# Attention softmax: the scaling of P by the inverse row sums, on ScalarE in place of VectorE

## The chip, the cores and the metric

One core of a Trainium2 chip. The metric is the device time of one execution in microseconds. All times below are of this kernel on this chip.

## The reference

The model is a "macaron" layer on 4 sequences of 256 tokens with hidden size 512: half a feed-forward step, attention, half a feed-forward step, each on a layer-normed input and added to x.

```python
x = x + 0.5 * ffn(layernorm(x))      # dense 512x512 + bias, LoRA with 8 experts of rank 16, top 2
x = x + attn(layernorm(x))           # 32 query heads, 8 key/value heads of 128, window of 128, rope
x = x + 0.5 * ffn(layernorm(x))
...
scores = einsum('bqhgd,bshd->bhgqs', qg, k) * sm_scale
allowed = (j <= i) & (j > i - 128)
attn = softmax(where(allowed, scores, neg), axis=-1)
out = einsum('bhgqs,bshd->bqhgd', attn, v).reshape(B, S, N_Q_HEADS * HEAD_DIM) @ wo
```

The part that the change touches is the division inside `softmax`: each row of exponentials is scaled by the inverse of its sum.

## The kernel before

Everything is fp32. To keep precision on a matrix engine that rounds its operands, each operand is split in a "hi" part (a rounded copy, made by ScalarE) and a "lo" part (the difference, made by VectorE or GpSimd), and each product is made of three passes.

**Loops.** The attention runs over 8 groups g (one key/value head with its 4 query heads). Each group has two halves (two sequences each), and each half 8 slots s: sequence b and query head h. That makes 128 units u. In a slot one head of one sequence goes through the softmax. Since the window is 128 and a sequence has two tiles of 128 queries, P of a unit is two tiles of 128x128: for the first query tile the causal block, for the second the causal block and the previous block folded in one by taking the element-wise minimum, because their allowed places don't overlap.

**Order of the work.** Nothing is scheduled by a tool: each engine has its own instruction list, written out slot by slot in a function `group(g, first, last)` of that engine, and runs it strictly in order. Semaphores tie the engines. The lists are skewed by a unit. In slot s, with u its unit:

- TensorE: nine matmuls of the next half's projections (`project`), `scores(u + 1)`, `p_transpose(u - 1)`; in slots 1 and 5 also `values`, in slots 2, 3, 6 and 7 `out_project`.
- VectorE: in slot 0 `v_lo`; in slots 0, 3, 4 and 7 `x_add`; then `softmax_norm(u)`; `rope_sum` and `rope_cos` in the slots in which a projection ends; `p_lo(u - 1)` (L827); `softmax_min(u + 1)` (L805 to L813); in slots 1 and 5 `o_lo`.
- ScalarE: `softmax_exp(u)` (L549, two exponentials of 128x128 with their row sums); in slot 0 `v_hi`; weight copies (`split_hi`, L495), before the rest in slots 4 and 7 of the first half, and some at the end of slots; `rope_swap` (L523, two copies of 64x512) in slots 1, 2, 3, 5 and 6, `v_copy` in slot 7; `p_hi(u - 1)` (L557); in slots 1 and 5 `o_hi`; then `rope_hi`.
- GpSimd: `rope_sin` (L365), `p_part(u - 1)` (L372, released by `p_lo`), `rope_lo` (L382), and weight differences (`split_lo`, L357), four of them for wo after slot 4 of the first half.
- SP issues the weight loads, each released by the differences that free its buffer.

The projections of a half end in slots 1, 2, 3, 5, 6 and 7, and that is where rope work of the list above stands.

**Around the change.** `exp_done`, `rinv_done` and `norm_done` count units. `p_transpose` waits for `norm_done`, `softmax_min(u + 1)` reads scores and writes `sm`, and the next `softmax_exp` waits for `min_done`. `prob`, `sm`, `rsum`, `rinv` and `nmax` have two buffers, taken by s % 2.

Of the kernel before, what the change touches and what calls it, by code (L numbers as in the profile page):

```python
# [22 lines left out]
ACT = mybir.ActivationFunctionType  # L23

P = 128
# [50 lines left out]
def macaron(nc, x_in, wq, wk, wv, wo, w_base, b_base, w_router, lora_a, lora_b, ident_in, mask_in, side_in, rope_in, out):  # L76
    ctx = ExitStack()
    with ctx:
# [29 lines left out]
        prob = sb("prob", [P, 2, 3 * P])  # L108
# [8 lines left out]
        rinv = sb("rinv", [P, 2, 2])  # L117
# [75 lines left out]
        rinv_done, norm_done = sem("rinv_done"), sem("norm_done")  # L193
# [242 lines left out]
        def _(act):  # L436
# [108 lines left out]
            def softmax_exp(u, s):  # L545
# [5 lines left out]
                                                accum_out=rsum[:, s % 2, i:i + 1])  # L551
                last.then_inc(exp_done, 1)

            def p_hi(u, s, beta):
                act.wait_ge(t_done, u + 1)
                wait(act, pv_done, 2 * beta)
                nc.scalar.activation(pT[0][:, 0:2, s % G, :], T[:, 0:2 * P].rearrange("p (c n) -> p c n", c=2),  # L557
                                     ACT.Copy).then_inc(pthi_done, 1)
# [8 lines left out]
            def group(g, first, last):  # L567
                for hf in range(2):
                    for s in range(SLOTS):
                        u, beta, b = 16 * g + 8 * hf + s, 4 * g + 2 * hf + s // G, s // G  # L570
                        start = first and hf == 0
                        softmax_exp(u, s)
                        if s == 0:
                            v_hi(2 * g + hf, hf)
                        weights(g, hf, s, last, (0, 1))
                        split, m = (ENDS.get(c) if not (last and hf == 1) else None for c in (s - 1, s))
                        if m == 5:
                            v_copy(2 * g + hf + 1)
                        elif m is not None:
                            rope_swap(2 * g + hf + 1, m)  # L580
                        if not (start and s == 0):
                            p_hi(u - 1, s - 1, beta - (s % G == 0))
                        if last and hf == 1 and s == 3:
                            x_hi(2, 0)
                            x_hi(2, 1)
                        if s % G == 1 and not (start and b == 0):
                            o_hi(beta - 1, (b + 1) % 2)
                        if split is not None and split < 5:
                            rope_hi(2 * g + hf + 1, split, 1 - hf)
                        weights(g, hf, s, last, (2, 3))  # L590
# [66 lines left out]
        def _(dve):  # L657
# [155 lines left out]
                nc.vector.tensor_tensor(sm[:, s % 2, P:2 * P], sm[:, s % 2, P:2 * P], sm[:, s % 2, 2 * P:3 * P],  # L813
                                        ALU.min).then_inc(min_done, 1)

            def softmax_norm(u, s):
                dve.wait_ge(exp_done, u + 1)
                nc.vector.reciprocal(rinv[:, s % 2, :], rsum[:, s % 2, :]).then_inc(rinv_done, 1)  # L818
                dve.wait_ge(rinv_done, u + 1)
                for i, (lo, hi) in enumerate(((0, P), (P, 2 * P))):  # L820
                    last = nc.vector.tensor_scalar(prob[:, s % 2, lo:hi], prob[:, s % 2, lo:hi],  # L821
                                                   rinv[:, s % 2, i:i + 1], None, ALU.mult)
                last.then_inc(norm_done, 1)

            def p_lo(u, s):
                dve.wait_ge(pthi_done, u + 1)
# [31 lines left out]
            def group(g, first, last):  # L858
                for hf in range(2):
                    for s in range(SLOTS):  # L860
                        u, beta, b = 16 * g + 8 * hf + s, 4 * g + 2 * hf + s // G, 2 * hf + s // G
                        start = first and b == 0
                        split, m = (ENDS.get(c) if not (last and hf == 1) else None for c in (s - 1, s))
                        if s == 0 and not (last and hf == 1):
                            v_lo(2 * g + hf, hf)
                        if s % G == 3 and not start:
                            x_add(beta - 1, (b - 1) % BATCH, 0)
                        if s % G == 0 and not (first and b < 2):
                            x_add(beta - 2, (b - 2) % BATCH, 1)
                        softmax_norm(u, s)  # L870
                        if split is not None and split < 5:
                            rope_sum(2 * g + hf + 1, split)
                        if m is not None and m < 5:
                            rope_cos(2 * g + hf + 1, m)
                        if not (start and s == 0):
                            p_lo(u - 1, s - 1)
                        if m == 5:
                            v_diff(2 * g + hf + 1)
                        if s == 0 and last and hf == 1:
                            v_lo(2 * g + hf, hf)  # L880
                        if not (last and hf == 1 and s == SLOTS - 1):
                            softmax_min(u + 1, (s + 1) % SLOTS)
                        if s % G == 1 and not start:
                            o_lo(beta - 1, (b + 1) % 2)
                        if last and hf == 1:
                            ffn_start(s)
# [415 lines left out]
```

## Time and profile before

| | us |
|---|---|
| median of 3 runs | 777.33 (776.9 to 781.51) |
| the profiled execution | 778.18 |
| its span, first to last instruction | 776.5 |
| TensorE, VectorE, ScalarE, GpSimd busy | 731.0, 643.7, 411.2, 392.9 |
| clock granted to TensorE, mean | 0.987 of full speed |

The profile is of one execution. Its time is 1.7 us longer than the span, for what lies before the first and behind the last instruction. A busy share is time with an instruction on the engine; matmuls overlap in the record, so a busy TensorE is not one at its peak. The attention stage runs from the first exponential at 96.31 us to the last at 725.94.

### The profile page before, as it was taken

The numbers are of one execution on the slowest core, as the hardware profiler recorded it, in microseconds if no ns is written. First come the engines' busy times: TensorE is split into PE (matmuls) and PEld (weight loads), VectorE is DVE, ScalarE is ACT, GpSimd is POOL, SyncE is SP. The second block draws the span as 40 slices with busy tenths as digits, with TensorE's granted clock in tenths as the row PEclk, the third lists the DMA queues.
The fourth block names the chain that finished last, engine by engine and source line by source line (L and its number), as shares of the span: only waits on it lengthen the run. The fifth ranks groups of instructions, "written<-read, shape, count | busy, mean of one in ns | idle before, by whom it ended". The sixth has DMA issues, their size and how long they took to land.

```text
span 776.5 us, 13949 instructions
## 1 busy us (share of the span) xinstructions
PE 731.0 (94%) x3692; PEld 606.8 (78%) x3692; DVE 643.7 (83%) x2060; ACT 411.2 (53%) x1122; POOL 392.9 (51%) x466
## 2 busy tenths in 40 slices
PE   5989878999899999999999999998999899988998
PEld 3878667888788877887788788887888788876876
DVE  3888879888888898878888888888878888898795
ACT  1333456655665566556565656565656655554311
POOL 0384537643764375537653665357634764462420
PEclk8899998999999999999999999999999999999999
DMA  9040002200210022001200120002100210020002
GB/s 298 1 177 14 1 0 69 69 1 1 68 56 14 0 68 54 14 0 54 68 14 0 30 80 24 0 5 90 41 0 0 73 49 0 2 109 0 1 29 82
DMA packets 25843, 32.13 MB, mean 41 GB/s; under 512 B 5833, under 2 KB 14281, under 8 KB 25298
## 3 DMA queue, kind: packets, MB, share of 16 engines
q1 hardware_dynamic: 21072, 30.43, 12.3%
q10 hardware_dynamic: 4738, 1.31, 0.8%
q8 instruction: 14, 0.23, 0.1%
q14 instruction: 19, 0.16, 0.1%
HBM read 27.54 MB, written 4.19 MB: 41 GB/s over the span
## 4 chain that ended last, share of the span: by engine, by line
PE 47%; DVE 31%; issue 10%; ACT 9%; ACTq 2%; DVEq 1%; POOL 0%
PE bank L1101 16%; PE bank L1159 12%; DVE sm L813 7%; PE bank L1144 5%; PE bank L1067 4%; ACT prob L549 4%; PE bank L1123 3%; DVE sm L806 3%; DVE rot L777 3%; DVE oT_lo L833 2%; DVE rot L786 2%; DVE pT_hi_lo L827 2%; DVE sm L805 2%; PE bank L1131 2%; ACTq L442 2%
## 5 line engine op out<-in xcount | busy, mean ns | idle before, releaser
L549 ACT ACTIVATE prob<-sm,nmax 128x128 f32<-128x128 f32 x256 | 101.1, 396 | 220.2 <-DVE sm L813 217.7
L365 POOL TENSOR_TENSOR swap<-swap,rope 128x512 f32<-128x512 f32 x80 | 104.9, 1311 | 151.2 <-ACT swap L523 151.2
L372 POOL TENSOR_SCALAR_AFFINE_SELECT pT_hi_lo<-pT_hi_lo 128x256 fp32r<-128x256 f32 x128 | 52.8, 413 | 145.8 <-DVE pT_hi_lo L827 145.0
L813 DVE TENSOR_TENSOR sm<-sm 128x128 f32<-128x128 f32 x128 | 112.1, 876 | 0.0
L523 ACT ACTIVATE swap<-bank 64x512 f32<-64x512 f32 x160 | 95.1, 594 | 9.5 <-PE bank L1101 6.7
L382 POOL TENSOR_TENSOR q_lo<-rot,q_hi 128x512 fp32r<-128x512 f32 x64 | 82.6, 1291 | 7.6 <-ACT q_hi L531 7.6
L821 DVE TENSOR_SCALAR prob<-prob,rinv 128x128 f32<-128x128 f32 x256 | 78.9, 350 | 4.5
L1159 PE MATMUL bank<-wo_hi,oT_hi 128*128 128x512 f32 x256 | 75.1, 415 | 5.0 <-DVE x L840 4.6
L1101 PE MATMUL bank<-xnT_hi,wq_hi 128*128 128x512 f32 x256 | 73.0, 398 | 2.9 <-DVE v_lo L797 1.3
L1101 PE MATMUL bank<-xnT_lo,wq_hi 128*128 128x512 f32 x256 | 73.9, 391 | 0.0
L1101 PE MATMUL bank<-xnT_hi,wq_lo 128*128 128x512 f32 x256 | 72.3, 395 | 0.0
L1159 PE MATMUL bank<-wo_lo,oT_hi 128*128 128x512 f32 x256 | 68.8, 390 | 0.0
L1159 PE MATMUL bank<-wo_hi,oT_lo 128*128 128x512 f32 x256 | 68.6, 390 | 0.0
L777 DVE TENSOR_TENSOR rot<-bank,rope 128x512 f32<-128x512 f32 x80 | 54.9, 687 | 12.9 <-ACT swap L523 12.9
L557 ACT ACTIVATE pT_hi_lo<-bank 128x256 fp32r<-128x256 f32 x128 | 48.9, 382 | 29.6 <-PE bank L1131 22.7
L1144 PE MATMUL bank<-pT_hi_lo,v_hi 128*128 128x512 f32 x192 | 62.1, 404 | 0.0
L1101 PEld LDWEIGHTS bank<-xnT_hi,wq_hi 128*128 128x128 f32 x256 | 47.8, 189 | 16.0 <-DVE rot L777 4.5
L818 DVE RECIPROCAL rinv<-rsum 128x2 f32<-128x2 f32 x128 | 20.6, 161 | 47.0 <-ACT prob L549 47.0
L827 DVE TENSOR_TENSOR pT_hi_lo<-bank,pT_hi_lo 128x256 fp32r<-128x256 f32 x128 | 53.4, 417 | 6.2 <-ACT pT_hi_lo L557 5.9
L1123 PE MATMUL bank<-k_hi_lo,q_hi 128*128 128x256 f32 x256 | 58.3, 310 | 0.0
L786 DVE TENSOR_TENSOR rot<-rot,swap 128x512 f32<-128x512 f32 x80 | 57.2, 716 | 0.0
L1159 PEld LDWEIGHTS bank<-wo_lo,oT_hi 128*128 128x128 f32 x256 | 48.1, 188 | 10.8
(148 smaller groups left out, 1724.1 us busy)
## 6 DMA issues: line engine op xcount, KB each, us to landing
raw<-in_L_attn_wq SPq DMA_DIRECT2D x32, 256.0 KB, 3.0
raw<-in_L_attn_wo SPq DMA_DIRECT2D x32, 256.0 KB, 2.7
x<-in_L_attn_x SPq DMA_DIRECT2D x4, 512.0 KB, 7.8
raw<-in_L_attn_wk SPq DMA_DIRECT2D x8, 256.0 KB, 2.6
raw<-in_L_attn_wv SPq DMA_DIRECT2D x8, 256.0 KB, 2.6
out<-x SPq DMA_DIRECT2D x8, 256.0 KB, 2.0
raw<-in_L_ffn_W_base ACTq DMA_DIRECT2D x4, 256.0 KB, 5.5
wb_keep_hi<-q_hi SPq DMA_DIRECT2D x1, 1024.0 KB, 5.0
```

Source lines behind the costliest of these rows:

```text
L365: nc.gpsimd.tensor_tensor(w, w, tab, ALU.mult).then_inc(t2_done, 1)
L382: nc.gpsimd.tensor_tensor(lo, rot[:, m % 2, :], hi.bitcast(F32), ALU.subtract).then_inc(qlo_done, 1)
L523: last = nc.scalar.activation(swap[a:a + half, m % 2, :], A[m % 2][b:b + half, :], ACT.Copy)
L549: last = nc.scalar.activation(prob[:, s % 2, lo:hi], sm[:, s % 2, lo:hi], ACT.Exp, bias=nmax[:, s % 2, i:i + 1], scale=-1.0, accum_out=rsu ...
L777: nc.vector.tensor_tensor(rot[:, m % 2, :].rearrange("p (b s) -> p b s", b=2), A[m % 2][:, :].rearrange("p (b s) -> p b s", b=2), rope[:, ...
L786: nc.vector.tensor_tensor(rot[:, m % 2, :], rot[:, m % 2, :], swap[:, m % 2, :], ALU.add).then_inc(sum_done, 1)
L813: nc.vector.tensor_tensor(sm[:, s % 2, P:2 * P], sm[:, s % 2, P:2 * P], sm[:, s % 2, 2 * P:3 * P], ALU.min).then_inc(min_done, 1)
L821: last = nc.vector.tensor_scalar(prob[:, s % 2, lo:hi], prob[:, s % 2, lo:hi], rinv[:, s % 2, i:i + 1], None, ALU.mult)
L1101: last = mm(A[m % 2][:, :], w, xnT[b][:, d, hf * HALF:(hf + 1) * HALF], start=(i == 0), stop=(i == 11))
L1123: last = mm(S[s % 2][:, 2 * P:4 * P], q[a][:, hf, h, q1], k[c][:, hf, b * SEQ:(b + 1) * SEQ], start=(n == 0), stop=(n == 2))
L1144: last = mm(O[i][:, :], v[a][:, par, 2 * b + kb, :], pT[c][:, blk, :, :], start=(n == 0), stop=(n == len(todo) - 1))
L1159: last = mm(C[:, :], oT[a][:, par, i, h, :], wo_s[c][:, h, :], start=(h == 0 and n == 0), stop=(h == G - 1 and n == 2))
```

## The change

The two scalings of a unit leave VectorE, where `softmax_norm` becomes `softmax_recip` with the reciprocal alone. ScalarE gets a `softmax_norm` of its own: it waits for the reciprocal and scales the two tiles in place, as copies with a scale read per partition from `rinv`. It stands in ScalarE's list behind the weight copies and behind `rope_swap` or `v_copy` of the slot, and ahead of `p_hi(u - 1)`. `norm_done` is now counted up by ScalarE. VectorE no longer waits for its own reciprocal.

```diff
--- before.py
+++ after.py
@@ -551,6 +551,13 @@
                                                 accum_out=rsum[:, s % 2, i:i + 1])
                 last.then_inc(exp_done, 1)
 
+            def softmax_norm(u, s):
+                act.wait_ge(rinv_done, u + 1)
+                for i, (lo, hi) in enumerate(((0, P), (P, 2 * P))):
+                    last = nc.scalar.activation(prob[:, s % 2, lo:hi], prob[:, s % 2, lo:hi], ACT.Copy,
+                                                scale=rinv[:, s % 2, i:i + 1])
+                last.then_inc(norm_done, 1)
+
             def p_hi(u, s, beta):
                 act.wait_ge(t_done, u + 1)
                 wait(act, pv_done, 2 * beta)
@@ -578,6 +585,7 @@
                             v_copy(2 * g + hf + 1)
                         elif m is not None:
                             rope_swap(2 * g + hf + 1, m)
+                        softmax_norm(u, s)
                         if not (start and s == 0):
                             p_hi(u - 1, s - 1, beta - (s % G == 0))
                         if last and hf == 1 and s == 3:
@@ -813,14 +821,9 @@
                 nc.vector.tensor_tensor(sm[:, s % 2, P:2 * P], sm[:, s % 2, P:2 * P], sm[:, s % 2, 2 * P:3 * P],
                                         ALU.min).then_inc(min_done, 1)
 
-            def softmax_norm(u, s):
+            def softmax_recip(u, s):
                 dve.wait_ge(exp_done, u + 1)
                 nc.vector.reciprocal(rinv[:, s % 2, :], rsum[:, s % 2, :]).then_inc(rinv_done, 1)
-                dve.wait_ge(rinv_done, u + 1)
-                for i, (lo, hi) in enumerate(((0, P), (P, 2 * P))):
-                    last = nc.vector.tensor_scalar(prob[:, s % 2, lo:hi], prob[:, s % 2, lo:hi],
-                                                   rinv[:, s % 2, i:i + 1], None, ALU.mult)
-                last.then_inc(norm_done, 1)
 
             def p_lo(u, s):
                 dve.wait_ge(pthi_done, u + 1)
@@ -867,7 +870,7 @@
                             x_add(beta - 1, (b - 1) % BATCH, 0)
                         if s % G == 0 and not (first and b < 2):
                             x_add(beta - 2, (b - 2) % BATCH, 1)
-                        softmax_norm(u, s)
+                        softmax_recip(u, s)
                         if split is not None and split < 5:
                             rope_sum(2 * g + hf + 1, split)
                         if m is not None and m < 5:
```

## Rows read from the trace of the kernel before

**Rows 1.** The page, part 1: busy us (share) and instructions of each engine.

```profile
PE 731.0 (94%) x3692; PEld 606.8 (78%) x3692; DVE 643.7 (83%) x2060; ACT 411.2 (53%) x1122; POOL 392.9 (51%) x466
```

**Rows 2.** Table by stretches, one group: start:end, us, then each engine's busy us.

```profile
260.60:340.94 80.34, 78.23 (x398) 65.36 (x397) 68.13 (x216) 48.16 (x133) 44.47 (x46) 1.00 0.11 33
```

**Rows 3.** Waits in that group: total us, times, longest.

```profile
ACT prob L549 <- DVE sm L813: 29.2, 17, 3.1
...
DVE rinv L818 <- ACT prob L549: 5.9, 10, 1.0
```

**Rows 4.** Timeline, ScalarE, second half, slot 1: start us, us, instruction.

```profile
302.58 0.40 ACT L549 ACTIVATE prob<-sm,nmax 128x128 f32<-128x128 f32 x1 [3.12 <-DVE sm L813]
...
302.89 0.19 ACT L549 ACTIVATION_READ_ACCUMULATOR prob<-sm,nmax 128x1 f32 x1
...
303.49 1.20 ACT L523 ACTIVATE swap<-bank 64x512 f32<-64x512 f32 x2
...
304.71 0.39 ACT L557 ACTIVATE pT_hi_lo<-bank 128x256 fp32r<-128x256 f32 x1
...
306.85 0.40 ACT L549 ACTIVATE prob<-sm,nmax 128x128 f32<-128x128 f32 x1 [0.78 <-DVE sm L813]
```

**Rows 5.** Timeline, VectorE, second half, slots 1 and 2.

```profile
303.49 0.17 DVE L818 RECIPROCAL rinv<-rsum 128x2 f32<-128x2 f32 x1 [0.95 <-ACT prob L549]
...
303.69 0.49 DVE L821 TENSOR_SCALAR prob<-prob,rinv 128x128 f32<-128x128 f32 x2
...
305.33 0.41 DVE L827 TENSOR_TENSOR pT_hi_lo<-bank,pT_hi_lo 128x256 fp32r<-128x256 f32 x1
...
309.73 0.42 DVE L827 TENSOR_TENSOR pT_hi_lo<-bank,pT_hi_lo 128x256 fp32r<-128x256 f32 x1
...
310.93 1.21 DVE L813 TENSOR_TENSOR sm<-sm 128x128 f32<-128x128 f32 x1
```

**Rows 6.** Timeline, GpSimd: wo in the first half, rope_lo in the second.

```profile
280.19 5.06 POOL L357 TENSOR_TENSOR wo_lo<-raw,wo_hi 128x512 fp32r<-128x512 f32 x4
...
310.70 1.29 POOL L382 TENSOR_TENSOR k_hi_lo<-rot,k_hi_lo 128x512 fp32r<-128x512 f32 x1
```

**Rows 7.** Timeline, ScalarE: first exponentials of slots (1, 2; 4 to 7; 3, 4).

```profile
260.59 0.40 ACT L549 ACTIVATE prob<-sm,nmax 128x128 f32<-128x128 f32 x1 [1.84 <-DVE sm L813]
...
265.14 0.41 ACT L549 ACTIVATE prob<-sm,nmax 128x128 f32<-128x128 f32 x1 [0.59 <-DVE sm L813]
...
275.74 0.41 ACT L549 ACTIVATE prob<-sm,nmax 128x128 f32<-128x128 f32 x1 [2.25 <-DVE sm L813]
...
280.41 0.40 ACT L549 ACTIVATE prob<-sm,nmax 128x128 f32<-128x128 f32 x1 [0.75 <-DVE sm L813]
...
286.67 0.41 ACT L549 ACTIVATE prob<-sm,nmax 128x128 f32<-128x128 f32 x1 [2.25 <-DVE sm L813]
...
292.02 0.40 ACT L549 ACTIVATE prob<-sm,nmax 128x128 f32<-128x128 f32 x1 [2.29 <-DVE sm L813]
...
312.17 0.40 ACT L549 ACTIVATE prob<-sm,nmax 128x128 f32<-128x128 f32 x1 [1.69 <-DVE sm L813]
...
317.45 0.40 ACT L549 ACTIVATE prob<-sm,nmax 128x128 f32<-128x128 f32 x1 [2.24 <-DVE sm L813]
```

**Rows 8.** Timeline, VectorE: slots 5 and 7, then slot 0 of the second half.

```profile
281.52 2.57 DVE L821 TENSOR_SCALAR prob<-prob,rinv 128x128 f32<-128x128 f32 x2
...
294.51 0.42 DVE L827 TENSOR_TENSOR pT_hi_lo<-bank,pT_hi_lo 128x256 fp32r<-128x256 f32 x1 [0.29 <-ACT pT_hi_lo L557]
...
299.56 0.15 DVE L818 RECIPROCAL rinv<-rsum 128x2 f32<-128x2 f32 x1
...
300.15 0.42 DVE L827 TENSOR_TENSOR pT_hi_lo<-bank,pT_hi_lo 128x256 fp32r<-128x256 f32 x1
```

**Rows 9.** Timeline, ScalarE: p_hi in slot 4, and two router copies at the end.

```profile
277.57 0.37 ACT L557 ACTIVATE pT_hi_lo<-bank 128x256 fp32r<-128x256 f32 x1
...
734.49 0.45 ACT L483 ACTIVATE ar_part<-bank 128x136 f32<-128x136 f32 x2
```

## The prediction

> **What bounds the kernel now.** I read four views in this order. The shares of busy time [rows 1] name TensorE first (94%), VectorE second (83%), with ScalarE half idle. That is the tempting reading: the change moves work from a full engine to an idle one. The table by stretches [rows 2] shows one pass of the head-group loop: 80.34 us, with the clock at its full level; TensorE is busy 78.23 of them, so 2.1 us a group is all that it would give back. The waits of the same stretch [rows 3] show what the averages hide: ScalarE's exponential waits 17 times, for 29.2 us, and always for the last VectorE operation of the minimum (L813); VectorE's reciprocal waits 10 times for the exponential (5.9 us). Last, the timelines [rows 4 to 9]: each slot is a loop over two engines, exp(u) on ScalarE, then scaling(u), p_lo(u-1) and minimum(u+1) on VectorE, then exp(u+1). The start of one exponential to the start of the next is the slot's time, and 16 such steps fill the 80.34 us. TensorE runs at most a slot ahead of this loop and waits for it now and then; the loop waits for TensorE only in slot 1 of the first half. So what counts is the step from exponential to exponential, not any engine's load.
>
> **What the change removes and adds.** Off VectorE go two scalings a slot, which take 0.48 us as a pair when nothing blocks them [rows 5], over 128 slots. On ScalarE come two ACTIVATEs of 128x128 with a scale read per partition, behind the bank copies (swap) or weight copies of the slot and ahead of p_hi(u-1), with a new wait on VectorE's reciprocal. Behind that wait on ScalarE are queued p_hi(u-1), o_hi, rope_hi and the second pair of weight copies; VectorE's p_lo(u-1) waits for p_hi, and minimum(u+1), the next exponential, x_add and rope_cos wait behind p_lo. No DMA moves: those issued by SP are released by the weight conversions, and these keep their order.
>
> **The price of the pair** is not in the trace, since no ACTIVATE with a pointer as scale and no sum stands there. Below: the two plain copies of 128x136 at the end take 0.45 us together [rows 9], and as an operation can start 0.09 before the end of the one ahead (302.58 + 0.40 against 302.89 [rows 4]) such a pair holds the queue 0.36 us. Above: two exponentials of this very shape, 0.40 each [rows 4], not overlapped, 0.81 us. The exponential is the nearer relative: same shape, same buffers, one pointer operand (its bias). Its accumulator read follows 0.31 us after its start (302.89 after 302.58 [rows 4]), and I take 0.30 a piece, 0.60 for the pair before p_hi can start. A price below nothing is excluded, since the pair only adds to ScalarE's list; what it takes off VectorE is counted separately.
>
> The Trainium skill ("ScalarE: Activation LUTs", What ACT_TABLE_LOAD costs) gives 186 ns plus 0.833 ns an element, 93 ns more for each pointer operand and 93 ns of overlap; an estimate by it is 386 ns an operation and 0.59 us for the pair, and the whole sum would stay as it is. Its table of rules says to multiply on VectorE and not on ScalarE, which speaks against this change; the 0.48 us of a pair on VectorE [rows 5] agree in direction.
>
> **Slots with a swap.** In the second half's slot 1 [rows 4, 5] the exponential starts at 302.58, the swap ends 2.13 later and p_hi starts there; VectorE meanwhile does reciprocal, scaling and rope_cos and starts p_lo at 2.75. So today's scaling stands fully beside the swap, and taking it away buys nothing. After the change ScalarE does swap (to 2.13), scaling (2.73), p_hi (0.39), and with 0.03 of hand-over (310.93 + 1.21 against 312.17 [rows 5, 7]) p_lo starts at 3.15. From p_lo to the next exponential it is 1.52 us when L813 runs freely (305.33 to 306.85 [rows 4, 5]), 2.44 when GpSimd's rope_lo holds it (309.73 to 312.17 [rows 5, 7]: L813 takes 1.21 us and ends 0.15 after the GpSimd operation [rows 5, 6]). Both tails begin at p_lo, since the GpSimd work is released by p_lo too, and move with it. New steps are 4.68 and 5.60. Slots 1 and 5 of the second half, built alike: 4.27 to 4.68, twice +0.41. Slot 1 of the first half, now 4.55 because of TensorE [rows 7]: +0.13. Slot 2 in both halves and slot 6 of the second, 5.32: three times +0.28. Slot 3 in both halves, 5.28: twice +0.32. Together +2.4.
>
> **Slots in which p_lo waits for p_hi already.** In the first half's slots 4 and 7 weight copies stand ahead of p_hi (277.57, 1.83 after the exponential [rows 7, 9]; in slot 7 p_lo idles 0.29 us for it [rows 8]). The pair goes in front one for one: twice +0.60. Slot 0 of each half is worst for a new reason: VectorE's reciprocal comes late (299.56, after v_lo and x_add), and ScalarE now stands at the new wait. Now p_lo starts 0.59 after the reciprocal [rows 8]; after it 0.20 + 0.60 + 0.42 = 1.22: twice +0.63. Slots 4 and 7 of the second half have neither swap nor late reciprocal: the scaling can start 1.1 after the exponential, 1.0 before a swap would let it, and p_lo then waits for rope_sum as long as for p_hi: nothing. Together +2.5.
>
> **The slot that gains.** In slot 5 of the first half the two scalings take 2.57 us instead of 0.48 [rows 8]: GpSimd runs four wo differences back to back, 280.19 to 285.25 [rows 6], and each scaling gets in only between two of them. On ScalarE they aren't held. p_lo would start 3.15 after the exponential; L813 would be ready at 280.41 + 3.15 + 1.20 = 284.8 (1.20 behind p_lo as at 310.93 [rows 5]), wait for the end of the wo work, end 0.15 later, and the exponential follows at 285.43: 5.02 in place of 6.26, -1.24. In slot 6 rope_lo, queued behind the late GpSimd work, then comes after L813, and the step is 4.68 in place of 5.35: -0.67. Together -1.9.
>
> The Trainium skill ("SBUF — State Buffer", SBUF: two separate sides) calls the port pair that GpSimd and VectorE share an exclusive lock held for a whole instruction; the 2.57 us agree. Its rule would count every scaling moved off VectorE as a relief, and that is the first rival below.
>
> **Sum.** 2.4 + 2.5 - 1.9 = +3.0 us a group. Six middle groups: 18.0. The first lacks p_lo in its slot 0 (-0.4 there) and TensorE's limit in slot 1: +2.9. The last gains 0.6 in its first half, where slot 7 has no weight copies; in its second the four slots up to the start of the dense stage lose 0.6 each (+2.4, an estimate: there p_lo comes right behind the scaling, and the pair and p_hi stand between), then TensorE alone is the bound and later slots cost nothing. In all 18.0 + 2.9 - 0.6 + 2.4 = +22.7 us. The execution profiled took 778.18 (span 776.5), so 800.9; it stood 0.85 above the median of 777.33, and against that the forecast is 800.0. The feed-forward stages before and after have none of the edited code: nothing. TensorE idles more (some 5 of 83 us a group), still mostly busy, and I count nothing for the clock.
>
> **Rivals.**
> First, faster: ScalarE hides the pair and TensorE becomes the bound. The place is slots 5 and 6, price -1.9 a group at once, and TensorE's 2.1 idle us [rows 2] are the floor: 7.8 groups of it, -16, 761 us. It decides if elsewhere p_lo isn't delayed, which needs a pair of 0.32 us or less (13 steps a group carry its length, so 0.01 us is 0.13 a group; break-even is near 0.37). For it: ScalarE is idle 32 of 80 us and the block is real. Against: p_hi starts the moment the swap ends, and 0.32 is below the bound from plain copies. 0.09.
> Second, no change: a cheap pair of 0.36 to 0.48 us, like the plain copies. 0.36 gives 0 a group, 0.48 gives 1.5: 776 to 790, mostly under 785. 0.14.
> Third, slower still: GpSimd work catches L813 anew. If L813 in slot 6 meets rope_lo, or in slot 5 rope_sin after wo, a held L813 costs 0.9 to 1.3 us a group, 7 to 10 in all: 808 to 813; with the pair at its upper bound of 0.81 it would be 825. In slot 6 the two stand within 0.1 us of each other in my reckoning. 0.16.
> Fourth, the change isn't what it says: the copy with a scale is built as something else, with a table load. The trace has copies and exponentials side by side without one. 0.01, far above the range.
> My forecast itself, 786 to 808: 0.60.
>
> **Range and chances.** 782 to 814 leaves out the faster rival, the bottom of the second, and the top of the third. A change of 1% (7.8 us) is about what a measurement of this kernel can tell from none. Faster by over 1%: 0.09. Within 1%, under 785: 0.13. Slower by over 1%: 0.78.
>
> **What would show it.** In the changed profile: L549 still waits for L813, some 83.3 us a group; p_lo (L827) waiting for p_hi in most slots, where it hardly waits now; ACTIVATEs of the scaling near 0.39 us, 0.30 apart; ScalarE waiting for the reciprocal in slot 0; no scaling on VectorE in slot 5 and a step near 5.0 there; TensorE's busy share down to some 91%. I am wrong if p_hi isn't delayed by the pair's length, if the pair costs under 0.4 us, or if L813 is held in other slots than now.

## The result and the profile after

The changed kernel takes 798.7 us (median of 4 runs, 798.61 to 799.1) against 777.5 on the same chip: 1.026 times the time before, 95% interval 1.023 to 1.030. The profiled execution took 798.73 with a span of 797.0, at the same mean clock (0.987). Forecast were 800.0, +22.7 us; measured are +21.2 on the medians, +20.5 on the spans.

Part 1 of the page of the changed kernel, its chain of work that ended last by engine, and two groups of its costliest instructions (L557 is the scaling on ScalarE, L830 `p_lo`, L564 `p_hi`, L826 the reciprocal, L821 the last operation of the minimum):

```profile
PE 739.7 (93%) x3692; PEld 607.0 (76%) x3692; DVE 573.3 (72%) x1804; ACT 482.7 (61%) x1378; POOL 397.8 (50%) x466
...
DVE 32%; ACT 31%; issue 21%; PE 12%; ACTq 3%; DVEq 1%; POOL 1%
...
L557 ACT ACTIVATE prob<-prob,rinv 128x128 f32<-128x128 f32 x256 | 88.8, 394 | 28.6 <-DVE rinv L826 26.7
...
L830 DVE TENSOR_TENSOR pT_hi_lo<-bank,pT_hi_lo 128x256 fp32r<-128x256 f32 x128 | 54.4, 425 | 68.5 <-ACT pT_hi_lo L564 68.5
```

The same line of the chain for the kernel before:

```profile
PE 47%; DVE 31%; issue 10%; ACT 9%; ACTq 2%; DVEq 1%; POOL 0%
```

VectorE lost 70 us of work against [rows 1], TensorE's share fell by a point, ScalarE still has 39% to spare, and the kernel is slower. What grew is ScalarE's part in the chain, from 9% to 31%; TensorE now holds 12% of it where it held 47%, and `p_lo` idles 68.5 us for `p_hi`.

The table by stretches for one group of the head-group loop, and its waits (total us, times, longest), to be laid beside [rows 2, 3]:

```profile
342.38:425.40 83.02, 79.36 (x397) 65.28 (x397) 59.40 (x184) 56.93 (x164) 45.16 (x46) 1.00 0.11 32
```

```profile
ACT prob L549 <- DVE sm L821: 22.4, 16, 2.5
...
DVE pT_hi_lo L830 <- ACT pT_hi_lo L564: 7.8, 16, 1.1
...
DVE rinv L826 <- ACT prob L549: 5.9, 10, 1.0
ACT prob L557 <- DVE rinv L826: 3.1, 3, 1.4
```

A group takes 83.02 us in place of 80.34. The loop still ends at the minimum. New are the 16 waits of `p_lo`, one in each slot (there were two, of 0.5 us in all, in the group of [rows 3]), and three of the scaling for the reciprocal. Timelines of the changed kernel, ScalarE and VectorE, in the second half's slots 0 and 1 (slot 1 is that of [rows 4, 5]):

```profile
386.78 0.69 ACT L557 ACTIVATE prob<-prob,rinv 128x128 f32<-128x128 f32 x2 [1.43 <-DVE rinv L826]
387.38 0.36 ACT L564 ACTIVATE pT_hi_lo<-bank 128x256 fp32r<-128x256 f32 x1
390.23 0.41 ACT L549 ACTIVATE prob<-sm,nmax 128x128 f32<-128x128 f32 x1 [2.49 <-DVE sm L821]
...
391.14 1.20 ACT L523 ACTIVATE swap<-bank 64x512 f32<-64x512 f32 x2
392.36 0.69 ACT L557 ACTIVATE prob<-prob,rinv 128x128 f32<-128x128 f32 x2
392.96 0.36 ACT L564 ACTIVATE pT_hi_lo<-bank 128x256 fp32r<-128x256 f32 x1
...
394.89 0.40 ACT L549 ACTIVATE prob<-sm,nmax 128x128 f32<-128x128 f32 x1 [0.59 <-DVE sm L821]
```

```profile
386.59 0.15 DVE L826 RECIPROCAL rinv<-rsum 128x2 f32<-128x2 f32 x1
387.77 0.43 DVE L830 TENSOR_TENSOR pT_hi_lo<-bank,pT_hi_lo 128x256 fp32r<-128x256 f32 x1 [1.03 <-ACT pT_hi_lo L564]
...
393.35 0.42 DVE L830 TENSOR_TENSOR pT_hi_lo<-bank,pT_hi_lo 128x256 fp32r<-128x256 f32 x1 [0.29 <-ACT pT_hi_lo L564]
```

In slot 1 the pair stands between swap and `p_hi` and holds the queue for 0.60 us (392.36 to 392.96), at 394 ns for each copy. The step from exponential to exponential is 4.66, where it was 4.27. In slot 0 ScalarE stands idle for 1.43 us until the reciprocal comes; then come 0.19 of hand-over, 0.60 for the pair, 0.39 for `p_hi`, and `p_lo` starts 1.18 after the reciprocal, 0.59 later than before [rows 8].

The sixteen steps of this group, from the first half's slot 1 on: 4.66, 5.57, 5.57, 5.26, 5.04, 4.66, 5.53; second half 6.24, 4.66, 5.56, 5.56, 4.55, 4.66, 5.57, 4.61; then slot 0 of the next first half, 5.33.

### The profile page after: what moved, and what is told of

It is laid out like the page before. It is cut to its first block, busy times and chain, and to the rows that moved or that the text cites. A ratio compares the mean times of both kernels' runs of the same rounds, so it can differ in the third digit from the quotient of the medians.

```text
span 797.0 us, 13949 instructions
## 1 busy us (share of the span) xinstructions
PE 739.7 (93%) x3692; PEld 607.0 (76%) x3692; DVE 573.3 (72%) x1804; ACT 482.7 (61%) x1378; POOL 397.8 (50%) x466
## 4 chain that ended last, share of the span: by engine, by line
DVE 32%; ACT 31%; issue 21%; PE 12%; ACTq 3%; DVEq 1%; POOL 1%
DVE sm L821 11%; ACT prob L549 9%; ACT prob L557 7%; ACT swap L523 6%; DVE sm L814 5%; ACT pT_hi_lo L564 4%; PE bank L1070 4%; DVE sm L813 4%; ACTq L442 1%; PE bank L1162 1%; DVE x L843 1%; DVE nmax L818 1%; PE bank L1147 1%; PE bank L1104 1%; DVE swap L697 1%
## 5 line engine op out<-in xcount | busy, mean ns | idle before, releaser
L365 POOL TENSOR_TENSOR swap<-swap,rope 128x512 f32<-128x512 f32 x80 | 104.2, 1303 | 146.1 <-ACT swap L523 146.1
L557 ACT ACTIVATE prob<-prob,rinv 128x128 f32<-128x128 f32 x256 | 88.8, 394 | 28.6 <-DVE rinv L826 26.7
L830 DVE TENSOR_TENSOR pT_hi_lo<-bank,pT_hi_lo 128x256 fp32r<-128x256 f32 x128 | 54.4, 425 | 68.5 <-ACT pT_hi_lo L564 68.5
L821 DVE TENSOR_TENSOR sm<-sm 128x128 f32<-128x128 f32 x128 | 102.8, 803 | 0.0
L785 DVE TENSOR_TENSOR rot<-bank,rope 128x512 f32<-128x512 f32 x80 | 55.3, 691 | 48.1 <-ACT swap L523 47.3
L1147 PE MATMUL bank<-pT_hi_lo,v_hi 128*128 128x512 f32 x192 | 64.5, 418 | 0.0
L1162 PEld LDWEIGHTS bank<-wo_hi,oT_hi 128*128 128x128 f32 x256 | 43.3, 188 | 27.8 <-issue 22.1
L1104 PEld LDWEIGHTS bank<-xnT_hi,wq_hi 128*128 128x128 f32 x256 | 47.3, 188 | 18.6 <-DVE rot L785 7.2
L794 DVE TENSOR_TENSOR rot<-rot,swap 128x512 f32<-128x512 f32 x80 | 59.8, 748 | 0.1
L1134 PE MATMUL bank<-ident,prob 128*128 128x128 f32 x256 | 49.1, 273 | 8.1 <-DVE pT_hi_lo L830 8.1
```

Of the source, the lines that this page charges most:

```text
L365: nc.gpsimd.tensor_tensor(w, w, tab, ALU.mult).then_inc(t2_done, 1)
L557: last = nc.scalar.activation(prob[:, s % 2, lo:hi], prob[:, s % 2, lo:hi], ACT.Copy, scale=rinv[:, s % 2, i:i + 1])
L785: nc.vector.tensor_tensor(rot[:, m % 2, :].rearrange("p (b s) -> p b s", b=2), A[m % 2][:, :].rearrange("p (b s) -> p b s", b=2), rope[:, ...
L794: nc.vector.tensor_tensor(rot[:, m % 2, :], rot[:, m % 2, :], swap[:, m % 2, :], ALU.add).then_inc(sum_done, 1)
L1104: last = mm(A[m % 2][:, :], w, xnT[b][:, d, hf * HALF:(hf + 1) * HALF], start=(i == 0), stop=(i == 11))
L1147: last = mm(O[i][:, :], v[a][:, par, 2 * b + kb, :], pT[c][:, blk, :, :], start=(n == 0), stop=(n == len(todo) - 1))
```

## The experiments

All times are medians of timed rounds, each beside the kernel before on the same chip, which took 777.3 to 777.4. Theory A is that of the prediction: the pair's length lies ahead of `p_hi` in ScalarE's strict order, so `p_lo`, the minimum and the next exponential move by it. The diffs are against the changed kernel unless another one is named; they are cut to the lines that matter, and their comments are added here.

**e3_plain_pair: a shorter pair in the same place.** The copies have no scale operand, so P isn't divided by its sums.

```diff
-    last = nc.scalar.activation(prob[...], prob[...], ACT.Copy, scale=rinv[:, s % 2, i:i + 1])
+    last = nc.scalar.activation(prob[...], prob[...], ACT.Copy)
```

> The changed kernel with plain copies in place (no scale operand), so P is not divided by its row sums; queue place and waits stay. It shortens the pair alone. Theory A with the size in the prediction (13 steps a group carry the pair's length, 0.01 us is 0.13 us a group): a plain copy of this shape takes about 0.29 us and starts 0.20 after the one ahead, the pair 0.40 in place of 0.60, so 2.6 us a group less, 8 groups: 778 to 781. Rival D (it is the new wait on the reciprocal and the hop between engines, not the length): unchanged, 797 to 799.

Measured: 778.64, ratio 1.001 (0.9998 to 1.0028). ScalarE's timeline in this kernel, with `p_hi` at L563:

```profile
361.22 1.20 ACT L523 ACTIVATE swap<-bank 64x512 f32<-64x512 f32 x2
362.44 0.51 ACT L557 ACTIVATE prob<-prob 128x128 f32<-128x128 f32 x2
362.86 0.36 ACT L563 ACTIVATE pT_hi_lo<-bank 128x256 fp32r<-128x256 f32 x1
```

The pair holds the queue for 0.42 us in place of 0.60, and the steps fall by the same 0.18 (4.66 to 4.48, 5.57 to 5.38). The instruction, its wait and its place are all still there, and 20 us are gone. The length does it. It also says where the pair would have been nearly free: the second rival was a pair as cheap as plain copies, and the scale operand alone carried it out of that case.

**e4_wait_alone: the wait without the pair.** Kernel before, with ScalarE waiting for the reciprocal ahead of `p_hi`.

```diff
+                        act.wait_ge(rinv_done, u + 1)
                         if not (start and s == 0):
                             p_hi(u - 1, s - 1, beta - (s % G == 0))
```

> The kernel before, with the new wait alone: VectorE scales as before, and ScalarE waits for the reciprocal at the place at which the change put it, with no scaling there. Theory A: in 14 of 16 slots the reciprocal is long done, and in slot 0 p_lo follows the scaling on VectorE anyway: 777 to 779, no change. Rival D: most of the loss shows here, 790 to 799.

Measured: 777.63, ratio 1.0003 (0.9993 to 1.0013). In slot 0 ScalarE does wait, up to 1.5 us, and next to nothing is late by it: the reciprocal starts 0.59 us before VectorE starts `p_lo` [rows 8], and the hand-over and `p_hi` alone just fit in between. The first half's slot 0 takes 4.84 in place of 4.73, and slot 1, which TensorE bounds, is shorter by the same 0.11; the second half's slot 0 takes 5.65 in place of 5.63.

**e7_longer: two plain copies ahead of the pair,** into a tile that nobody reads.

```diff
+                for lo, hi in ((0, P), (P, 2 * P)):
+                    nc.scalar.activation(spare[:, lo:hi], prob[:, s % 2, lo:hi], ACT.Copy)
                 for i, (lo, hi) in enumerate(((0, P), (P, 2 * P))):
```

> The changed kernel with two more ACTIVATEs of 128x128 in front of each pair, plain copies of P to a tile that nothing reads. From the changed kernel and e3, the pair's length counts in 13 to 15 steps a group; two plain copies add 0.39 us of queue time. Theory A: 5 to 6 us a group, 8 groups, less at the ends: 836 to 846. If ScalarE's length were hidden in part beyond some point: under 825.

Measured: 847.31, ratio 1.090 (1.088 to 1.092), a little over the forecast. Its timeline on ScalarE (L558 the added copies, L560 the scaling, L567 `p_hi`):

```profile
414.38 0.51 ACT L558 ACTIVATE spare<-prob 128x128 f32<-128x128 f32 x2
414.80 0.68 ACT L560 ACTIVATE prob<-prob,rinv 128x128 f32<-128x128 f32 x2
415.38 0.36 ACT L567 ACTIVATE pT_hi_lo<-bank 128x256 fp32r<-128x256 f32 x1
```

The added copies hold the queue for 0.42 us, and 15 of 16 steps grow by 0.37 to 0.41. Slot 5 of the first half doesn't (5.04 to 5.06): there the minimum had waited for the end of GpSimd's wo work (0.67 us in the changed kernel), and the longer pair only uses up that slack. 15 steps of 0.395 are 5.9 us a group, as the group shows (88.94 from 83.02), so 46 over 7.8 groups. The span grew by 47.3, and 46.5 of it lie between the first and the last exponential; the 48.6 of the medians are above that because the profiled execution was the shortest of its four (846.02). 15 slots carry the added length, and not the 13 of the prediction: slots 4 and 7 of the second half do so too (4.55 to 4.95, 4.62 to 5.02).

**e1_behind_phi and e2_behind_all: the same pair in another place.** Behind `p_hi`, and behind `p_hi`, `o_hi` and `rope_hi`.

```diff
-                        softmax_norm(u, s)
                         if not (start and s == 0):
                             p_hi(u - 1, s - 1, beta - (s % G == 0))
+                        softmax_norm(u, s)          # e1
...
                             rope_hi(2 * g + hf + 1, split, 1 - hf)
+                        softmax_norm(u, s)          # e2
```

> The changed kernel with one line moved: on ScalarE the scaling of unit u stands behind p_hi(u-1) and no longer ahead of it. The engine that scales, the pair's length and the wait on the reciprocal stay. Theory A (the loss is the place: the pair lies between swap and p_hi, and p_lo waits for p_hi): p_hi starts at the swap's end again, 2.13 us after the exponential, p_lo starts at 2.75 with rope_cos as its last predecessor. Steps from exponential to exponential then sum to about 76 us a group, under TensorE's 78.2 of work, so TensorE is the bound: 758 to 768 us, faster than before (777.5) by 1 to 2%. Rival B (the loss is ScalarE's extra work and the hop VectorE to ScalarE, wherever it stands): 795 to 800, no better than the changed kernel. Rival C (only the slots with late reciprocals and weight copies recover): 780 to 790.

> As e1, but the scaling stands behind o_hi and rope_hi too, as late in ScalarE's list as it can before the second pair of weight copies. Theory A: what matters is that p_hi isn't held, and TensorE reads the scaled P only a slot later, so the same as e1 within 2 us, 758 to 768. Where o_hi or rope_hi matter (o_lo and GpSimd's rope_lo wait for them) this is up to 3 us better than e1; if TensorE's transposes wait for the late scaling it is worse, by 1 to 5 us, and TensorE would be seen idle at L1134's line for the scaling. Rival B: 795 to 800.

Measured: 757.84, ratio 0.975 (0.973 to 0.976), at the lower edge of its band, and 753.63, ratio 0.970 (0.968 to 0.971), 4.4 us below its band and 4.2 better than e1_behind_phi, where up to 3 were expected. The steps that differ most in the groups read are slots 4 and 7 of the first half and slot 4 of the second, each shorter by 0.18 to 0.20; the cause wasn't followed. The same instructions on the same engine, later in its list, turn 2.6% slower into 3.0% faster. A group of e2_behind_all in the table by stretches, its chain by engine, its waits in that group, and ScalarE in the second half's slot 1:

```profile
325.12:402.48 77.36, 77.23 (x397) 65.48 (x397) 59.45 (x184) 57.19 (x165) 44.80 (x46) 1.00 0.12 34
```

```profile
PE 81%; DVE 9%; ACT 5%; issue 2%; ACTq 2%; POOL 1%; DVEq 0%
```

```profile
ACT prob L549 <- DVE sm L821: 17.0, 16, 1.7
```

```profile
370.45 1.19 ACT L523 ACTIVATE swap<-bank 64x512 f32<-64x512 f32 x2
371.67 0.38 ACT L564 ACTIVATE pT_hi_lo<-bank 128x256 fp32r<-128x256 f32 x1
371.95 1.08 ACT L571 ACTIVATE oT_hi<-bank 128x512 fp32r<-128x512 f32 x2
372.90 0.70 ACT L557 ACTIVATE prob<-prob,rinv 128x128 f32<-128x128 f32 x2
373.81 0.40 ACT L549 ACTIVATE prob<-sm,nmax 128x128 f32<-128x128 f32 x1 [0.21 <-DVE sm L821]
```

The pair now lies in time that ScalarE spent waiting for the minimum, TensorE is busy for all of the group but 0.13 us, and 81% of the chain is TensorE's. The expectations had put TensorE's floor near 78.2 us a group (761 in all by the prediction's first rival), because that was its busy time in [rows 2]. It was too high by 0.9. TensorE's busy time is no fixed need: the same 3692 matmuls are counted busy for 731.0 us in the kernel before, 739.7 in the changed one and 723.7 in e2_behind_all, at mean clocks of 0.987 to 0.989. Which records stretch, and why, wasn't followed.

**e6_no_scaling: no scaling on any engine;** P isn't divided by its sums, and TensorE's transposes wait for the reciprocal.

```diff
-                        softmax_norm(u, s)
...
-                pe.wait_ge(norm_done, u + 1)
+                pe.wait_ge(rinv_done, u + 1)
```

> The changed kernel with the scaling left out on every engine (P is not divided by its row sums); TensorE's transposes wait for the reciprocal. It shows what taking the scaling off VectorE is worth with no price on ScalarE. Theory A: TensorE is the bound, and e2, which took 753.6, hides the ScalarE pair fully: 752 to 755. Rival F (the pair still costs in e2, in o_hi, rope_hi or the next exponential): 5 us or more under e2.

Measured: 752.94, ratio 0.969 (0.967 to 0.970), within 0.7 us of e2_behind_all. That is the floor, and a pair at the end of ScalarE's list costs next to nothing above it.

**e11_slot0: only slot 0 of each half mended.** There the pair goes behind `p_hi`.

```diff
-                        softmax_norm(u, s)
+                        if s:
+                            softmax_norm(u, s)
                         if not (start and s == 0):
                             p_hi(u - 1, s - 1, beta - (s % G == 0))
+                        if s == 0:
+                            softmax_norm(u, s)
```

> The changed kernel, with the scaling behind p_hi in slot 0 of each half alone. It takes out the new wait on the late reciprocal, and leaves the pair ahead of p_hi in the other 14 slots. The slots 0 took 6.23 and 5.33 us in the changed kernel and would take 5.1 and 4.5 as p_lo then waits for the reciprocal alone; the other steps stay: 1.9 us a group less, 782 to 786. If the loss were mostly this wait: under 779; if slot 0 didn't matter: 796 to 799.

Measured: 785.29, ratio 1.011 (1.009 to 1.012). Moving the pair in two slots of 16 wins back 13.4 of the 21.2 us. Their steps fall from 6.24 and 5.33 to 5.09 and 4.46, which is also below the 5.63 and 4.72 of before: with the pair behind `p_hi`, slot 0 keeps what VectorE's lighter list saves between reciprocal and `p_lo`. So not all of the 13.4 was loss: against the kernel before, the two slots had cost 0.61 each, 1.2 us a group. And slot 1 of the first half, which TensorE bounds, gives back 0.16 (4.66 to 4.82).

**e9_slots56: the term that gains, by itself.** Kernel before, with ScalarE's scaling in slots 5 and 6 of the first half only.

```diff
+                        if hf == 0 and s in (5, 6):
+                            softmax_norm(u, s)      # ScalarE, ahead of p_hi
...
-                        softmax_norm(u, s)
+                        softmax_norm(u, s, here=not (hf == 0 and s in (5, 6)))   # VectorE
```

> The kernel before, with the scaling on ScalarE in slots 5 and 6 of the first half, at the place at which the change put it; VectorE scales in the other 14. With slot 5 alone on ScalarE (e5) the step of slot 5 fell to 5.04 us as forecast, but slot 6 rose from 5.35 to 7.46: VectorE came 1.2 us earlier, its scaling then met GpSimd's wk work (1.55 us in place of 0.51) and rope_sum met rope_sin (1.79 in place of 0.69). Theory A with this added: with slot 6's scaling off VectorE too, rope_sum slips in before wk as in the changed kernel, slot 6 takes 4.7, and the 1.9 us a group of the prediction are there: 760 to 765. Rival E (an early VectorE is caught in slot 6 or 7 whatever it runs): 778 to 790.

Measured: 762.98, ratio 0.983 (0.981 to 0.985). The steps are 5.05 and 4.67, as forecast (5.02 and 4.68).

**e5_slot5: slot 5 alone.** The same with `s == 5` in both conditions.

> The kernel before, with the scaling on ScalarE in slot 5 of the first half alone, at the place at which the change put it; in the other 15 slots of a group VectorE scales. Theory A (relief in this one slot, loss in the others): the step of slot 5 falls from 6.27 to 5.04 us and that of slot 6 from 5.35 to 4.8 to 5.0 (VectorE's scaling of slot 6 may meet GpSimd's late work), 1.5 to 1.8 us a group until TensorE is the bound: 763 to 768 us. Rival E (GpSimd's wo work catches another VectorE operation for as long, so there is nothing to win): 775 to 778.

Measured: 789.39, ratio 1.016 (1.014 to 1.017). A miss by over 21 us, and in sign. Timelines of VectorE, GpSimd and TensorE in its slot 6 (L832 the scaling, L795 rope_sum, L365 rope_sin, L851 `x_add`, L1170 `out_project`):

```profile
371.58 1.55 DVE L832 TENSOR_SCALAR prob<-prob,rinv 128x128 f32<-128x128 f32 x2
373.05 1.79 DVE L795 TENSOR_TENSOR rot<-rot,swap 128x512 f32<-128x512 f32 x1
```

```profile
371.75 1.29 POOL L357 TENSOR_TENSOR wk_lo<-raw,wk_hi 128x512 fp32r<-128x512 f32 x1
373.00 1.29 POOL L365 TENSOR_TENSOR swap<-swap,rope 128x512 f32<-128x512 f32 x1
```

```profile
378.47 1.92 PE L1170 MATMUL bank<-wo_hi,oT_hi 128*128 128x512 f32 x4 [2.15 <-DVE x L851]
```

And the table by stretches around that wait of TensorE (start:end, us, busy us of each engine, then the granted clock):

```profile
376.00:378.00 2.00, 0.33 (x2) 0.09 (x2) 1.96 (x7) 0.24 (x1) 1.58 (x2) 1.00 0.00 0
378.00:381.00 3.00, 2.53 (x6) 2.04 (x7) 2.33 (x8) 3.00 (x10) 0.16 (x1) 0.60 0.00 0
```

Slot 5 fell to 5.06 as wanted. But VectorE was then early for slot 6, where its scaling now met the wk difference (1.55 us in place of 0.51) and rope_sum met rope_sin (1.79 in place of 0.68). Slot 6 took 7.45 in place of 5.35, and slot 0 of the second half 6.56 in place of 5.63. TensorE, which waited 2.15 us for `x_add`, came back at a clock of 0.60, near the lower of its two levels (1.2 GHz), and in slot 0 of the second half its transposes are late: `p_hi` idles 2.20 us for them, where it idled 0.76 before. How much of this is the wait itself and how much the clock wasn't separated. Slot 7's own step stayed at 4.93. The changed kernel's group shows 1.00. Against e9_slots56, which moves one slot more, the difference is 26 us. The relief of slot 5 is worth something only if the scaling of slot 6 leaves VectorE as well.

**e8_vector_late: the good place, on VectorE.** Kernel before, with the scaling behind the minimum.

```diff
                             softmax_min(u + 1, (s + 1) % SLOTS)
+                        softmax_norm(u, s)          # VectorE; the reciprocal stays ahead
```

> The kernel before with the scaling kept on VectorE, but moved behind minimum(u+1) (the reciprocal stays), so that it runs beside the next exponential. Theory A, that the place in the list counts and not the engine: faster than before. Slot 0 gains 0.4 us in each half, slots 4 and 7 of the second half 0.4 each, slot 5 of the first half 1.2, and slot 6 loses up to 0.5 where GpSimd holds the late scalings and o_lo behind them: 762 to 770. Rival G, that only the move to the idle engine can win: 775 to 780.

Measured: 842.28, ratio 1.083 (1.081 to 1.084), a miss by over 70 us. VectorE, GpSimd and TensorE in its slots 4 and 5:

```profile
387.01 2.50 DVE L823 TENSOR_SCALAR prob<-prob,rinv 128x128 f32<-128x128 f32 x2
...
394.22 0.42 DVE L829 TENSOR_TENSOR pT_hi_lo<-bank,pT_hi_lo 128x256 fp32r<-128x256 f32 x1 [4.05 <-ACT pT_hi_lo L557]
```

```profile
386.90 5.00 POOL L357 TENSOR_TENSOR wo_lo<-raw,wo_hi 128x512 fp32r<-128x512 f32 x4
```

```profile
389.57 0.44 PE L1134 MATMUL bank<-ident,prob 128*128 128x128 f32 x2 [2.82 <-DVE prob L823]
```

`p_lo` releases GpSimd's work, so behind `p_lo` and the minimum is where GpSimd is busy. The scaling is held there for 2.50 us, TensorE's transposes wait for it, and all behind them. The clock adds to it; the table by stretches of the same place:

```profile
386.00:390.00 4.00, 1.18 (x9) 0.88 (x8) 4.00 (x5) 2.27 (x7) 4.00 (x4) 1.00 0.14 46
390.00:394.00 4.00, 4.00 (x12) 3.13 (x12) 0.17 (x1) 0.19 (x1) 3.13 (x3) 0.57 0.60 208
```

After its 2.82 us of waiting TensorE runs the products with v at 0.57 of full clock, and `p_hi` and `p_lo` wait for those: `p_lo` idles 4.05 us. The step is 8.64 us. Slots 5 and 6 are 4.0 of the 8.4 us by which a group is longer than before (88.8 from 80.4); the largest of the others is slot 1 of the second half, with 1.7. How much of it all is the clock and how much the blocks themselves wasn't separated in this kernel.

**e10_late_both: that, with slots 4 to 6 of the first half on ScalarE** behind `rope_hi`.

```diff
+                        if hf == 0 and s in (4, 5, 6):
+                            softmax_norm(u, s)      # ScalarE, behind rope_hi
```

> Scaling behind minimum(u+1) on VectorE as in e8 (842.3), but in slots 4, 5 and 6 of the first half, where GpSimd's wo and wk work holds VectorE, on ScalarE behind rope_hi. In e8 the two steps of slots 5 and 6 took 8.64 and 6.97 us: the late scaling of slot 4 waited 2.5 us for wo, TensorE's transposes waited for it, and p_lo 4.05 us for them. Theory A (the place off the loop counts, on either engine, as long as nothing holds it): slots 5 and 6 fall to 5.0 and 4.7, TensorE is the bound: 752 to 764. Rival G (a late scaling on VectorE costs in all slots): over 775.

Measured: 800.87, ratio 1.031 (1.029 to 1.033), a miss by over 35 us. Slots 5 and 6 fell to 5.05 and 4.62. The late scalings of the slots that stayed met other GpSimd work; VectorE in the second half's slot 0 and TensorE in slot 1 behind it:

```profile
304.50 1.48 DVE L832 TENSOR_SCALAR prob<-prob,rinv 128x128 f32<-128x128 f32 x2
```

```profile
306.04 0.44 PE L1144 MATMUL bank<-ident,prob 128*128 128x128 f32 x2 [1.87 <-DVE prob L832]
```

In this group the clock fell behind that wait (0.62 over the next 4 us) and slot 1 took 7.23. The same wait, 1.85 to 1.87 us, stands in seven groups; in five of them the clock stayed at 1.00 and slot 1 took 5.95 to 5.98, against 4.27 in e2_behind_all. So the block and the late transposes are most of the loss, and the clock adds 1.1 to 1.3 us where it falls.

**e12_late_clear: ScalarE wherever GpSimd is busy,** that is slots 4 to 7 of the first half and 0 to 2 of the second; VectorE late in the others.

```diff
-                        if hf == 0 and s in (4, 5, 6):
+                        if hf == 0 and s > 3 or hf == 1 and s < 3:
```

> The kernel before, with the scaling on VectorE behind the minimum in the slots where GpSimd held nothing there (3 to 7 of the second half, 0 to 3 of the first), and on ScalarE behind rope_hi in the others (4 to 7 of the first half, 0 to 2 of the second). Theory A, that a late scaling on either engine is free as long as nothing holds it: every slot then costs what it costs with the scaling at the end of ScalarE's list, TensorE is the bound, 752 to 762 us, within some 1% of that kernel's 753.6. Rival, that a late VectorE scaling is bad in itself, by the length it adds between the minimum and the next reciprocal, so that blocks simply turn up in other slots: 780 us or more, as the run with ScalarE in slots 4 to 6 alone (800.9).

Measured: 765.17, ratio 0.986 (0.983 to 0.989): 3 us above the band of Theory A, far below the rival's. No scaling is held any more; the pairs on VectorE take 0.47 to 0.48 in the group read. What is left against e2_behind_all is 1.5 us a group (78.88 to 77.36), most of it in slot 5 of the second half (5.09 to 4.27) and slot 0 of the first (5.36 to 4.71); I read the former. VectorE, TensorE and ScalarE in this kernel's second half, slots 4 and 5:

```profile
392.50 1.19 DVE L822 TENSOR_TENSOR sm<-sm 128x128 f32<-128x128 f32 x1
393.61 0.47 DVE L832 TENSOR_SCALAR prob<-prob,rinv 128x128 f32<-128x128 f32 x2
```

```profile
394.13 0.44 PE L1144 MATMUL bank<-ident,prob 128*128 128x128 f32 x2 [0.67 <-DVE prob L832]
```

```profile
396.86 0.38 ACT L564 ACTIVATE pT_hi_lo<-bank 128x256 fp32r<-128x256 f32 x1 [1.03 <-PE bank L1157]
```

A minimum that GpSimd holds hands its delay to the scaling behind it, the transposes wait 0.67 us for that, the products with v come late, and so does `p_hi`: a step of 5.09 in place of 4.27. So a late scaling on VectorE has a price of its own where the minimum ahead of it is held. Theory A as I had put it, that either engine is as good while nothing holds the scaling itself, is only nearly true.

## Why the prediction was right

**The bound** was read rightly. VectorE's busy time fell by 70 us and the kernel became slower; e1_behind_phi and e2_behind_all show that ScalarE's load is not it either. One of the things to look for was off: TensorE's share is 93% and not some 91%, because its busy time grew by 8.7 us with the same matmuls.

**The price of the pair**: taken 0.60 us and 0.39 an operation, measured 0.60 and 0.394. The exponential of the same shape with one pointer operand was the right relative. Plain copies hold the queue for 0.18 less, and that is the whole 20 us (e3_plain_pair): at 0.42 the change costs 1.3 us. The break-even, put at 0.37, is so near 0.41. Two things moved it: at 0.60 a middle group grew by 2.7 and not 3.0, and the 0.18 less took 2.6 off it, which is 14 slots' worth and not 13. Slot 4 of the second half carries the length too (4.37 at 0.42, 4.55 at 0.60), slot 6 of the first hardly (4.63 and 4.66 in the group read).

**Slots with a swap**: forecast steps 4.68, 5.60 and 5.60, measured 4.66, 5.57 and 5.57. The 0.02 to 0.03 lie in `p_hi`, which takes 0.36 us right behind another ACTIVATE and not 0.39.

**Slots in which `p_lo` waits already**: twice +0.60 and twice +0.63 forecast; +0.59 in slots 4 and 7, +0.61 in both slots 0. Slots 4 and 7 of the second half: 4.55 where it was 4.55, and 4.62 as before.

**The slot that gains**: -1.24 and -0.67 forecast, -1.23 and -0.69 measured, and worth -14.3 us by themselves (e9_slots56). VectorE and GpSimd in the changed kernel, slots 5 and 6:

```profile
373.10 0.67 DVE L821 TENSOR_TENSOR sm<-sm 128x128 f32<-128x128 f32 x1
...
375.04 0.78 DVE L794 TENSOR_TENSOR rot<-rot,swap 128x512 f32<-128x512 f32 x1
...
378.14 0.29 DVE L821 TENSOR_TENSOR sm<-sm 128x128 f32<-128x128 f32 x1
```

```profile
368.53 5.08 POOL L357 TENSOR_TENSOR wo_lo<-raw,wo_hi 128x512 fp32r<-128x512 f32 x4
373.57 1.34 POOL L365 TENSOR_TENSOR swap<-swap,rope 128x512 f32<-128x512 f32 x1
...
375.24 1.73 POOL L357 TENSOR_TENSOR wk_lo<-raw,wk_hi 128x512 fp32r<-128x512 f32 x1
...
378.66 1.28 POOL L382 TENSOR_TENSOR q_lo<-rot,q_hi 128x512 fp32r<-128x512 f32 x1
```

The minimum ends 0.16 us behind the wo work, as reckoned. In slot 6 rope_sum (L794) got in 0.2 us ahead of GpSimd's wk difference, and this time GpSimd was the one held (1.73 in place of 1.29). That made all its later work late by 0.44: the minimum (378.14) ran freely, 0.52 ahead of rope_lo (378.66), where without the hold it would have been 0.1 ahead. So in the middle groups the third rival's block was as near as reckoned and didn't come. In the last group it did: there no wk difference follows the wo work, rope_lo is on time (709.92 to 711.20), the minimum ready at 710.16 meets it and takes 1.18 us, and slot 6 takes 5.56. Against the kernel before that slot grew by 0.24 where -0.67 was forecast. That the block stayed away from the middle groups so clearly is in part luck: the reckoning left 0.1 us, and the other 0.4 came from a hold that it hadn't foreseen. e5_slot5 shows what such meetings cost when they come in every group. The forecast price of the block was a little high: 7 to 10 us on 800 are 807 to 810, not 808 to 813, and a pair of 0.81 would by 13 steps of 0.21 give 821, not 825.

**Sum.** By the spans, +20.5: +2.94 in the first group from slot 1 on (forecast 3.3 there, -0.4 ahead of it, and -0.54 came ahead of it), +16.3 in the six middle groups (18.0), +3.3 in the last group and the dense stage behind it (1.8), -0.2 in the tail, and -1.3 before the attention, in a stage without edited code. That is a difference between runs: the first exponential of the fourteen kernels starts between 94.75 and 96.50, and the kernel before, at 96.31, is near the late end. From the first exponential to the last the loss is 22.0. A middle group grew by 2.7 and not 3.0: the eight slots with a swap ahead of the pair came out 0.02 to 0.04 shorter than forecast, 0.2 in all, and the rest lies in pieces of 0.01 or 0.02. The last group's term was the one sized worst, +1.5 off. Of this, 0.7 lie in its first half (+0.1 where -0.6 was forecast, by the block in slot 6) and 0.8 in the second (+3.2 where +2.4 was forecast): slot 1 grew by 0.97 and not 0.6, behind a 1.82 us wait of TensorE and a clock of 0.57, and slot 6, counted as free, by 0.45. The total came out so near because this term's 1.5 too little and the middle groups' 1.7 too much nearly cancel.

**Rivals.** The first failed as argued, since the pair is too long for its place by 0.28 us; its floor was itself too high, by the busy time taken for TensorE's need. That the wait for the reciprocal is by itself the cost is excluded by e4_wait_alone, and that the hop between the engines is, by e2_behind_all, which has it too.

## What to carry to other kernels

Where engines run lists in strict order, the place of an instruction in its list counts as well as its engine: find the loop that passes between the engines, and put added work behind the last instruction of its engine that this loop needs, here 45 us (798.7 to 753.6) between two places of one pair. The engine still counts in the good place: late on VectorE, where GpSimd's work held it, the same scaling took 842.3. An idle engine is no room if the idle time lies on the other side of that instruction.

Moving an operation out of the way of another engine's block pays only if the time that it frees doesn't bring the next operation under the next block. Walk at least two steps on before counting a relief, as the difference between e5_slot5 and e9_slots56 shows.

## What the runs showed of the hardware

The granted clock fell within the loop behind waits of TensorE: 0.57 to 0.58 in the 4 us behind each wait of 2.8 us (middle groups of e8_vector_late), 0.57 to 0.63 behind each of 2.14 or 2.15 (seven groups of e5_slot5). Behind waits of 1.85 to 1.87 us, which stand in the same slot of seven groups of e10_late_both, it fell twice (0.61 and 0.64) and stayed at 1.00 five times. The length of one wait doesn't decide it alone: in the changed kernel's first group one of 2.48 us left it at 1.00, and one of 2.19, 5 us later, was followed by 0.60. The seven groups also give the price of a fall, since the wait in them is the same: slot 1 took 7.23 and 7.05 us with it and 5.95 to 5.98 without. In the middle groups of the changed kernel no wait of TensorE reached 0.8 us, and the clock of each was 1.00.

A pair of 128x128 copies on ScalarE holds its queue for 0.42 us without and for 0.60 with a scale read per partition (0.51 and 0.69 from first start to last end). The Trainium skill ("ScalarE: Activation LUTs", What ACT_TABLE_LOAD costs) has 93 ns for each pointer operand; the two runs, e3_plain_pair and the changed kernel, agree, with 0.09 us an operation.

The blocks between VectorE and GpSimd work in both directions. VectorE's pair of 128x128 scalings takes 0.48 us alone and up to 2.57 [rows 5, 8] next to GpSimd's 128x512 operations; one of those takes 1.29 alone and 1.73 when rope_sum was there first. The Trainium skill ("SBUF — State Buffer", SBUF: two separate sides) calls it an exclusive lock on the port pair, and the stretched times on either side agree with that.
